# Twelve sets of gather buffers fewer in the last stage of an attention and mixture-of-experts kernel

## The reference

```
x = x + attention(layernorm(x), ctx)          # 32 heads of 16, keys and values shared by groups of 4
h = layernorm(x)
scores = softmax(h @ gate.T)                  # 8 experts; the two best of the two best groups, weights w1, w2
routed = w1 * expert_a(h) + w2 * expert_b(h)  # expert(h) = (silu(h @ g.T) * (h @ u.T)) @ d.T, inner width 352
shared = (silu(h @ sg.T) * (h @ su.T)) @ sd.T # inner width 704, for every token
x = x + routed + shared
```

## Time and profile before

| | us |
|---|---|
| median of 3 runs | 788.58 |
| the 3 runs | 787.97, 788.58, 791.93 |
| the profiled execution | 791.93 |
| its span, first to last instruction | 790.1 |
| PE busy in the span | 760.1 (96%) |
| DVE busy | 579.7 (73%) |
| ACT busy | 429.3 (54%) |
| POOL busy | 269.3 (34%) |
| gathers of the last stage, first and last start | 706.7 and 777.7 |

### The profile page before, as it was taken

How to read it: one execution, slowest core, us unless ns; L and a number is a source line. 1 busy time by engine, 2 the same in 40 slices (tenths; PEclk the granted TensorE clock), 3 DMA queues, 4 the chain that set the end, 5 groups by cost and what they waited for, 6 DMA issues and landing times.

```text
span 790.1 us, 16078 instructions
## 1 busy us (share of the span) xinstructions
PE 760.1 (96%) x5151; PEld 407.0 (52%) x5152; DVE 579.7 (73%) x1194; ACT 429.3 (54%) x843; POOL 269.3 (34%) x224
## 2 busy tenths in 40 slices
PE   6998999999999989999999999999999999999897
PEld 4553533343433325656755556555555555555553
DVE  4777779999999976998789886555555555547666
ACT  3666579999999973566433553434344343322231
POOL 3263008999993301665300101111111111015331
PEclk9999989999999999999999999999999999999999
DMA  8898846556645798998598576876777777559985
GB/s 330 324 405 245 250 139 211 185 168 194 195 121 172 228 331 295 331 376 275 173 232 225 137 173 137 187 174 175 183 175 180 179 180 173 126 164 288 288 240 150
DMA packets 161782, 172.07 MB, mean 218 GB/s; under 512 B 103680, under 2 KB 117504, under 8 KB 161216
## 3 DMA queue, kind: packets, MB, share of 16 engines
q1 hardware_dynamic: 150012, 128.89, 56.5%
q0 software_dynamic: 11120, 41.43, 16.8%
q10 hardware_dynamic: 596, 1.07, 0.4%
HBM read 105.40 MB, written 42.73 MB: 187 GB/s over the span
## 4 chain that ended last, share of the span: by engine, by line
PE 77%; DVE 10%; DMA 7%; ACT 2%; issue 2%; SPq 1%; DVEq 0%; ACTq 0%
PE psum L1467 29%; PE psum L1479 15%; PE psum L1317 8%; PE psum L1303 6%; PE psum L1231 4%; PE psum L1403 4%; PE psum L1207 4%; PE psum L1334 2%; DMA sb_weights<-in_wdn 2%; DMA sb_weights<-attn_dram 2%; PE psum L1183 1%; DMA sb_hT<-sb_h 1%; DMA sb_weights<-x_dram 1%; DMA sb_weights<-in_ctxT 1%; DVE sb_rows L1902 1%
## 5 line engine op out<-in xcount | busy, mean ns | idle before, releaser
L1467 PE MATMUL psum<-sb_weights,sb_rows 128*128 (+1 forms) x1608 | 250.8, 313 | 0.5 <-DMA sb_rows<-xnT_dram 0.5
L1467 PEld LDWEIGHTS psum<-sb_weights,sb_rows 128*128 128x128 f16 x1608 | 157.2, 98 | 91.8 <-DMA sb_rows<-xnT_dram 1.0
L1027 ACT ACTIVATE sb_weights<-psum,sb_rows 128x512 f32<-128x512 f32 x256 | 158.3, 683 | 16.9 <-PE psum L1303 15.0
L1699 DVE TENSOR_REDUCE sb_rows<-psum 128x4 f32<-128x1024 f32 x128 | 149.9, 1213 | 5.5 <-PE psum L1231 5.5
L1479 PE MATMUL psum<-sb_weights,sb_hT 128*128 (+1 forms) x630 | 147.4, 379 | 2.2 <-DMA sb_hT<-sb_h 2.2
L894 POOL DMA_INDIRECT sb_rows<-xn_rows,sb_slot_tok x39 | 38.2, 980 | 218.1 <-DVE sb_rows L2288 147.9
L1479 PEld LDWEIGHTS psum<-sb_weights,sb_hT 128*128 128x128 f16 x630 | 61.4, 98 | 67.5 <-DMA sb_hT<-sb_h 3.1
L1303 PE MATMUL psum<-sb_weights 50*128 50x512 f16 x256 | 90.0, 391 | 3.0 <-ACT sb_weights L1027 2.6
L1096 ACT ACTIVATE psum<-psum 128x352 f32<-128x352 f32 x71 | 31.8, 448 | 111.8 <-DVE psum L1949 111.8
L1317 PE MATMUL psum<-sb_weights 128*32 128x256 f32 x1024 | 82.9, 396 | 0.0
L1231 PE MATMUL psum<-sb_weights 48*128 48x256 f16 x512 | 73.2, 275 | 0.5 <-DVE sb_rows L1699 0.4
(11 more groups left out here) (264 smaller groups left out, 1017.9 us busy)
## 6 DMA issues: line engine op xcount, KB each, us to landing
sb_weights<-in_wgu SPq DMA_DIRECT2D x20, 704.0 KB, 7.4
sb_weights<-in_wgu POOLq DMA_DIRECT2D x20, 704.0 KB, 5.6
sb_weights<-in_wdn SPq DMA_DIRECT2D x17, 768.0 KB, 5.9
slot_y<-sb_rows SPq DMA_DIRECT2D x39, 256.0 KB, 2.3
sb_weights<-q_parts SPq DMA_DIRECT2D x96, 64.0 KB, 2.2
x_dram<-sb_rows SPq DMA_DIRECT2D x24, 256.0 KB, 4.6
q_parts<-sb_weights SPq DMA_DIRECT2D x16, 256.0 KB, 4.6
sb_rows<-in_x POOLq DMA_DIRECT2D x16, 256.0 KB, 4.8
```

Source lines behind the costliest of these rows:

```text
L1027: nc.scalar.activation(probs[G % 2][:, kt, pair * 512:(pair + 1) * 512], bank[4 + f % 2], ACT.Exp, scale=exp_scale[:, n:n + 1]).then_inc(e ...
L1467: mm = nc.tensor.matmul(bank[GU_BANKS[par][which]][:, 0:F], x_T[:, xp * D + k * P:xp * D + (k + 1) * P], gu(wp, k, which), start=(k == 0 a ...
L1699: nc.vector.tensor_reduce(to[:, :, j // UB, :, j % UB, qt], psum[:, banks[qt] * 512:(banks[qt] + 2) * 512] .rearrange("p (a h k) -> p a h ...
```

## The change

The 16 sets of buffers become 4 that are used in turn: 12 tiles of 128 by 512 words in place of 48. Since tile q is stored out of `gather_2[q % 4]`, the gathers of q >= 4 now wait until the store of tile q - 4 has landed (`out_st`), where they waited until DVE had finished it (`out_done`). All semaphores count the same; on SP and DVE no wait and no instruction is added, removed or moved, only the buffers' numbers differ.

```
-        gather_1, gather_2, res_out = [[words((TILES * j + q) * D, D) for q in range(TILES)] for j in range(3)]
+        gather_1, gather_2, res_out = [[words((4 * j + q) * D, D) for q in range(4)] for j in range(3)]
...
             def load_res(t, q):
-                sp.dma_start(res_out[q], tile_of(x2_dram, t)).then_inc(cx2_ld[q % 4], 16)
+                sp.dma_start(res_out[q], tile_of(x2_dram, t)).then_inc(cx2_ld[q], 16)
...
             def store_pair(m, side):
-                store_out(m + side * EARLY, late_done(m) if side else early_done(m), 2 * m + side)
+                store_out(m + side * EARLY, late_done(m) if side else early_done(m), 2 * (m % 2) + side)
...
             for q in range(2 * EARLY):
-                t, m = q // 2 + q % 2 * EARLY, q // 2 - 2
+                t, buf = q // 2 + q % 2 * EARLY, q % 4
                 if q >= 4:
-                    pool.wait_ge(out_done, (late_done(m) if q % 2 else early_done(m)) + 1)
+                    pool.wait_ge(out_st[buf], OUT_SEEN[buf] + 16 * (q // 4))
                 elif q > 0:
                     pool.wait_ge(u_ready, C0 + 2 + q)
-                for to, idx in ((gather_1[q], p1_i), (gather_2[q], p2_i)):
+                for to, idx in ((gather_1[buf], p1_i), (gather_2[buf], p2_i)):
                     nc.gpsimd.indirect_dma_start(
                         out=to, out_offset=None, in_=slot_y,
-                        in_offset=bass.IndirectOffsetOnAxis(ap=idx[:, t:t + 1], axis=0)).then_inc(gat_ld[q % 4], 16)
+                        in_offset=bass.IndirectOffsetOnAxis(ap=idx[:, t:t + 1], axis=0)).then_inc(gat_ld[buf], 16)
...
             def early_out(m, half):
 
-                q, n = 2 * m, m // 2
-                dve.wait_ge(cx2_ld[q % 4], n * 16 + (16 + CX2_SEEN))
-                dve.wait_ge(gat_ld[q % 4], n * 32 + 32)
+                q, n = 2 * (m % 2), m // 2
+                dve.wait_ge(cx2_ld[q], n * 16 + (16 + CX2_SEEN))
+                dve.wait_ge(gat_ld[q], n * 32 + 32)
```

More of the change, by code:

```diff
@@ L678, in load_res @@
             def load_res(t, q):
-                sp.dma_start(res_out[q], tile_of(x2_dram, t)).then_inc(cx2_ld[q % 4], 16)
+                sp.dma_start(res_out[q], tile_of(x2_dram, t)).then_inc(cx2_ld[q], 16)
             def store_out(t, done, q):
                 sp.wait_ge(out_done, done + 1)
-                sp.dma_start(tile_of(out_tiles, t), gather_2[q]).then_inc(out_st[q % 4], 16)
+                sp.dma_start(tile_of(out_tiles, t), gather_2[q]).then_inc(out_st[q], 16)
             def slot_rows(m, s):
@@ L707, in store_pair @@
             def store_pair(m, side):
-                store_out(m + side * EARLY, late_done(m) if side else early_done(m), 2 * m + side)
+                store_out(m + side * EARLY, late_done(m) if side else early_done(m), 2 * (m % 2) + side)
             def load_pair(m, side):
                 if m < EARLY:
-                    load_res(m + side * EARLY, 2 * m + side)
+                    load_res(m + side * EARLY, 2 * (m % 2) + side)
             for w in range(C0, TOTAL):
@@ L741, in _ @@
             store_pair(EARLY - 2, 1)
+            q = 2 * ((EARLY - 1) % 2) + 1
             sp.wait_ge(y_evac, TOTAL)
-            sp.dma_start(tile_of(out_tiles, TILES - 1), gather_2[TILES - 1]).then_inc(out_st[3], 16)
+            sp.dma_start(tile_of(out_tiles, TILES - 1), gather_2[q]).then_inc(out_st[q], 16)
             for q in range(4):
@@ L2329, in early_out, with late_sum @@
                                                    ALU.mult, ALU.add).then_inc(out_done, 1)
-            def late_sum(m, c):
-                q, n = 2 * m + 1, m // 2
+            def late_sum(m, c, q, n):
                 if c == 0:
-                    dve.wait_ge(cx2_ld[q % 4], n * 16 + (16 + CX2_SEEN))
+                    dve.wait_ge(cx2_ld[q], n * 16 + (16 + CX2_SEEN))
                 else:
@@ L2340, in late_out @@
             def late_out(m):
-                q, n, t = 2 * m + 1, m // 2, m + EARLY
+                q, n, t = 2 * (m % 2) + 1, m // 2, m + EARLY
                 dve.wait_ge(y_evac, m * 2 + (C0 + 2))
-                dve.wait_ge(gat_ld[q % 4], n * 32 + 32)
+                dve.wait_ge(gat_ld[q], n * 32 + 32)
                 nc.vector.scalar_tensor_tensor(res_out[q], gather_1[q], w1[:, t:t + 1], res_out[q],
@@ L2372, in _ @@
             late_low(1, 0)
-            late_sum(0, 0)
+            late_sum(0, 0, 1, 0)
             late_factor(1, 0)
@@ L2377, in _ @@
             late_low(1, 1)
-            late_sum(0, 1)
+            late_sum(0, 1, 1, 0)
             late_factor(1, 1)
@@ L2381, in _ @@
             for m in range(2, EARLY):
+                q, n = 2 * ((m - 1) % 2) + 1, (m - 1) // 2
                 late_unit(m, 0)
@@ L2384, in _ @@
                 late_low(m, 0)
-                late_sum(m - 1, 0)
+                late_sum(m - 1, 0, q, n)
                 late_factor(m, 0)
@@ L2397, in _ @@
                 late_low(m, 1)
-                late_sum(m - 1, 1)
+                late_sum(m - 1, 1, q, n)
                 late_factor(m, 1)
@@ L2402, in _ @@
             nc.vector.tensor_copy(hT[0][:, 1, :, :], last_hT[1]).then_inc(h_cut, 1)
-            m, q = last, TILES - 1
-            dve.wait_ge(cx2_ld[q % 4], m // 2 * 16 + (16 + CX2_SEEN))
-            dve.wait_ge(gat_ld[q % 4], m // 2 * 32 + 32)
+            m = last
+            q, n = 2 * (m % 2), m // 2
+            dve.wait_ge(cx2_ld[q + 1], n * 16 + (16 + CX2_SEEN))
+            dve.wait_ge(gat_ld[q + 1], n * 32 + 32)
             link = chain(links4 + late_done(m - 1) + 1)
-            link(nc.vector.scalar_tensor_tensor(res_out[q], gather_1[q], w1[:, TILES - 1:TILES], res_out[q],
+            link(nc.vector.scalar_tensor_tensor(res_out[q + 1], gather_1[q + 1], w1[:, TILES - 1:TILES], res_out[q + 1],
                                                 ALU.mult, ALU.add))
-            link(nc.vector.scalar_tensor_tensor(gather_2[q], gather_2[q], w2[:, TILES - 1:TILES], res_out[q],
+            link(nc.vector.scalar_tensor_tensor(gather_2[q + 1], gather_2[q + 1], w2[:, TILES - 1:TILES], res_out[q + 1],
                                                 ALU.mult, ALU.add))
@@ L2413, in _ @@
                     dve.wait_ge(y_evac, TOTAL - 1)
-                add_down(TOTAL - 2 + c, (C0 + c) % 2, (C0 + c) % 2, gather_2[q])
+                add_down(TOTAL - 2 + c, (C0 + c) % 2, (C0 + c) % 2, gather_2[q + 1])
 def _inputs(x, ctx, Wq, Wk, Wv, Wfc, bfc, gate, gate_w, up_w, down_w, sh_gate, sh_up, sh_down):
```

## The result

| | median us | runs |
|---|---|---|
| kernel before | 790.37 | 20 |
| changed kernel | 795.53 | 20 |
| ratio, changed to before | 1.0067 (95% interval 1.0044 to 1.0092) | |

The change costs 5.2 us where 0.2 was forecast; the time lies above the stated range. The price happens to be that of the first rival, but its mechanism is not what the runs show. In a second series of 12 runs the changed kernel came out at 1.0057 (1.0028 to 1.0085).

What follows compares the result with a forecast made beforehand. PE, with 77% of the chain, was taken as the bound, so only late gathers matter. Terms -0.7 + 0 + 0.9 = +0.2 us gave 788.8 from the median 788.58, forecast as 789.0; range 786.2 to 793.0.

Steps and rivals of the forecast that it cites:

- the first rival: Gathers late at every tight place, q = 6 and q = 15: 793.8 us, slower by 0.7%; chance 0.16.
- the one on q = 10, 12 and 14: Even q held by late q ahead still land before DVE wants them, least margin 1.9 us at q = 14; cost 0.
- the prediction's own signs of being wrong: DVE idling for gathers at q = 8, 10, 12 or 14, or a time outside 786.2 to 793.0.
- 2.1 for q = 13: Delay added to the start of q = 13's gathers, 765.43 to 767.5, when working out when q = 14 lands.
- A few us cost it nothing: Late tiles q = 5 to 13, fetched two tiles ahead, can start later; they matter only by holding back even q.
- The crowded stretch: Around 724 to 742, q = 6's gathers go out later but leave the jam: -0.7 us, ends -2.2 and +3.0.
- The stall near 732: PE idle 2.21 us until 734.32 for a transpose that took 9.19 us; the change could gain at most 2.2 us.
- q = 15 at the end: Last tile's second gather goes out 2.2 us later and all lateness reaches the end: +0.9 us, 0 to +2.2.
- The rule of the Trainium skill: Fixed part about 2.0 us plus bytes over 436 GB/s, 2.6 us per store: +0.3 at the end, nothing lost before.
- PE is unbroken between 745 and 773: Sign expected in the changed trace: PE has no idle time over these middle tiles of the last stage.
- the relief case: Rival: transpose near 732 and q = 6 land on time, q = 15 not late; -2.2 us, 786.4; chance 0.14.
- stands for the five: Pair of q = 9, starting at 743.34, taken as typical of late tiles q = 5, 7, 9, 11, 13.

Runs made afterwards that it cites:

- e7_9to14: Kernel before with sixteen buffers, but POOL waits for the landed store for q = 9 to 14 alone; ratio 1.0045 to the kernel before.
- e3_odd: Kernel before with sixteen buffers, but POOL waits for the landed store for odd q alone; ratio 1.0058 to the kernel before.
- e6_to8: Kernel before with sixteen buffers, but POOL waits for the landed store for q = 4 to 8 alone; ratio 0.9995 to the kernel before.
- e5_only15: Kernel before with sixteen buffers, but POOL waits for the landed store for q = 15 alone; ratio 1.0021 to the kernel before.
- e1: Kernel before with sixteen buffers, but POOL waits for the landed store for q = 4 to 15; ratio 1.0057 to the kernel before.
- e2: Changed kernel with gather_2 sixteen deep and POOL waiting for DVE's signal as before; ratio 0.9989 to the kernel before.
- e11: Kernel before, no store waits; gathers of q = 9, 11, 13 held until PE finished the second unit's gate and up; ratio 1.0055.
- e12: Changed kernel, but POOL takes q = 10 before 9, 12 before 11, 14 before 13; ratios 1.0002 and 0.9985 to the kernel before.
- e4_even: Kernel before with sixteen buffers, but POOL waits for the landed store for even q alone; ratio 1.0011 to the kernel before.

## Why the prediction was wrong

The step that failed is the one on q = 10, 12 and 14 with its sentence "Cost 0". It asked whether each gather lands before DVE wants it. That was mostly right: in the second profile of the changed kernel DVE waited for a gather only 0.96 us at early tile 3 and 1.07 us at the last tile, besides 0.84 at early tile 0, which both kernels have. (In the first, the gathers of q = 14, issued at 770.86 and 772.12, were 2.89 us late for DVE at 780.07. That is one of the prediction's own signs of being wrong, but PE was waiting for a transpose until 780.57, and not for DVE.) What the step left out is what the moved gathers do to others. It had even computed that q = 9 moves by the store's landing and that q = 10 goes out right behind; it did not lay this burst over SP's queue, where the second unit's transpose stands, though the chain had shown this very kind of transfer at 9.19 us with the DMA engines full, against 4.2 at 749.54. The term was taken as 0 and measures about +3.6 us (e7_9to14, 1.0045).

Point by point:

- The wait was right in kind: gathers start when the store lands, and the idle time ahead of POOL's gathers is now ended by a store (5.70 us in the row at 743.44). Its size was right at the end (2.2 us ahead of q = 15) and too small in the middle: the stores ahead of q = 9, 11 and 13 took 3.2, 4.7 and 4.8 us in the second profile, and the prediction counted 2.1 for q = 13.
- "A few us cost it nothing", of the odd q, was right for DVE and wrong for the kernel; by e3_odd they carry the loss.
- The crowded stretch, where the prediction put its effort (-0.7, ends -2.2 and +3.0), measures 0.9995, -0.4 us with an interval of some 2.4 us to either side. q = 6 was late by 0.85 and 0.96 us in the changed kernel's profiles, against 0.7 worked out, and by 2.92 in that of e6_to8. The stall near 732 was not a fixture: the second profile of the kernel before has none.
- q = 15 at the end: in the second profile the gather is what DVE now waits for, by 1.07 us, where it had waited 0.46 us for the residual. The net, some 0.6 us, stands beside the +0.9 forecast. In the first profile PE was later than this gather and DVE did not wait for it. The timed e5_only15 (1.0021) agrees with both numbers and with nothing.
- The first rival had the size (+5.2 us) by luck: it summed lateness of q = 6 and q = 15, of which the first is no cost that e6_to8's times show.
- The rule of the Trainium skill that was weighed (page "DMA: Bandwidth & Descriptors", section "Anatomy of one DMA — SWDGE (gpsimd) path", about 2.6 us for each store) is no better a guide here. The section fits transfers that GpSimd issues, while the stores are issued by SP; those of the second changed profile took 2.2 to 4.8 us between 735 and 782, against the 2.6 us of the estimate from that page. And what counted was not the length of the stores alone.
- "PE is unbroken between 745 and 773" was named as the sign to look for. It failed, at 754.33 and 766.95.
- Of the prediction's working, two things do not hold as written: its range starts at 786.2 and calls this the relief case, which its own sum puts at 786.4; and the q = 9 that "stands for the five" late tiles was checked against DVE's use alone.

Shown are: the wait is the cause (e1, e2), in q = 9 to 14 and the odd q (times), the moment of issue is enough (e11), and freeing the held pair removes it with the waits left in (e12, twice). Shown in three traces of the changed wait (both profiles and e1) is that the transposes of the second units of tiles 4 to 6 take 5.6 to 9.5 us, where they took 3.6 to 5.9 with the wait of the kernel before, and that PE idles for some of them (three, two and one). Open is the link in one place: the profiled executions of e3, e7 and e11 were among their fastest and have no idle PE in the middle tiles, so that their longer executions lose in the same way is inferred from the time and from transposes at 5.5 to 7.0 us against the margin of 7.0, not seen.

## What to carry to other kernels

Before moving a transfer, check not only whether it still lands in time for its own reader, but which transfer on the critical path it will now go out in front of, and how much margin that one has; here 2.8 us of it were used up by gathers that nobody was waiting for yet. When buffers are released in one order and refilled by a queue in another, a longer wait on one holds back those that are free: write the refills in the order of release. A difference of half a percent needs several series of runs and more than one profile, since a profiled execution may be one in which the loss does not occur.

## What the runs showed of the hardware

The granted clock of PE fell to its lower level (0.5, 1.2 GHz) right after some of the longer PE waits, inside a stage that otherwise ran at full clock. In e4_even PE waited 3.08 us and then took 3.23 us for nine products that take 2.1 (timeline of PE, then the row of the stretch with its clock):

```profile
732.78 3.23 PE L1482 MATMUL psum<-sb_weights,sb_hT 128*128 128x512 f16 x9 [3.08 <-DMA sb_hT<-sb_h]
```

```profile
733.70:737.00 3.30, 3.30 (x11) 1.36 (x10) 2.61 (x7) 1.11 (x3) 0.79 (x1) 0.50 1.08 217
```

The changed kernel's first profile has the same after its 2.45 us wait at 780.62: eighteen products in 5.75 us, where the kernel before took 4.24; the clock stood at 0.50 from 782 to 785. In e12_order it came after the 2.22 us at 747.52. The waits of 2.21 us in the kernel before and of 2.24 us in e11_delay were not followed by it. In e4_even the gate and up product behind the nine took 4.35 us in place of 3.74 as well, so a wait of PE can cost 1.5 to 1.7 us more than its own length. This may be one reason why single executions of these kernels differ by several us; no run here sets it apart.

Transfers landed later where more of them were in flight. A store of 256 KB took 2.0 to 3.6 us in the calm stretch and 5.1 to 7.1 in the crowded one. The transpose of unit (6, 1) took 3.6 us in the kernel before and 9.52 in the changed one; the DMA share was 0.50 from 771.2 to 776.7 there and 1.04 from 771.0 to 780.6 here.
